# A store on SyncE's queue that waits for a load on GpSimd's queue (fp32 decoder layer, one core)

## What is computed

```python
x = _rmsnorm(hidden_states, ln_weight)
h_q = (x @ w_q.T).reshape(b, lq, H, DH)
h_k = (key_value_states @ w_k.T).reshape(b, lk, H, DH)
h_v = (key_value_states @ w_v.T).reshape(b, lk, H, DH)
score = jnp.einsum('bqhd,bkhd->bhqk', h_q, h_k)
...
attn = jnp.einsum('bhqk,bkhd->bqhd', score, h_v).reshape(b, lq, H * DH)
out = attn @ w_out.T
```

## Time and profile before

| | |
|---|---|
| timed runs | 1069.12, 1069.39, 1070.8 us; median 1069.39 |
| profiled execution, its own time | 1065.68 us |
| its span, first to last instruction | 1063.5 us |
| TensorE busy | 1025.7 us (96% of the span) |
| VectorE, ScalarE, GpSimd busy | 761.1, 500.7, 472.9 us |
| DMA | 158.72 MB, mean 149 GB/s |

### The profile page before, as it was taken

The page is one execution under the profiler, slowest core; times in us unless marked ns, Lnnn a source line. Parts: engine busy times, 40 slices in busy tenths (PEclk is TensorE's granted clock), DMA queues, the critical chain, the costliest instruction groups (busy, mean ns, idle before and its releaser), DMA issues.

```text
span 1063.5 us, 20567 instructions
## 1 busy us (share of the span) xinstructions
PE 1025.7 (96%) x6354; PEld 890.7 (84%) x6354; DVE 761.1 (72%) x2269; ACT 500.7 (47%) x1377; POOL 472.9 (44%) x568
## 2 busy tenths in 40 slices
PE   7899978999989999999999999999999999999998
PEld 6677766888878888898888888888888888888786
DVE  6799989674657675767767676767676767676784
ACT  4888886463434353444343434444343434353422
POOL 7576676599954242423334242424242424242052
PEclk9999999999999999999999999999999999999999
DMA  4302001144275647373736464646464655635102
GB/s 155 130 12 61 2 1 60 66 149 176 87 241 181 216 144 237 123 245 139 251 130 235 147 222 168 223 151 224 162 221 144 217 178 182 209 131 200 68 1 80
DMA packets 44844, 158.72 MB, mean 149 GB/s; under 512 B 4736, under 2 KB 21504, under 8 KB 32128
## 3 DMA queue, kind: packets, MB, share of 16 engines
q0 software_dynamic: 14240, 103.82, 28.1%
q1 hardware_dynamic: 30560, 54.37, 15.3%
HBM read 148.73 MB, written 9.44 MB: 149 GB/s over the span
## 4 chain that ended last, share of the span: by engine, by line
PE 78%; DVE 9%; issue 5%; POOL 4%; ACT 3%; DMA 1%; POOLq 0%; DVEq 0%; ACTq 0%
PE bank L1948 25%; PE bank L760 20%; PE bank L2110 16%; PE bank L2097 5%; PE bank L2080 5%; PE bank L2128 3%; PE bank L2087 2%; DVE sm L481 2%; POOL sm L322 1%; DMA ring<-block_sums 1%; ACT pr L410 1%; PE bank L2166 1%; DVE alpha L557 1%; PE bank L686 1%; ACT pr L1341 0%
## 5 line engine op out<-in xcount | busy, mean ns | idle before, releaser
L1341 ACT ACTIVATE pr<-sm,nmx 128x128 f32<-128x128 f32 x256 | 99.8, 391 | 174.5 <-DVE nmx L1597 174.4
L1048 POOL TENSOR_TENSOR bm<-mask,bias 128x512 f32<-128x512 f32 x64 | 84.6, 1323 | 160.7 <-DVE nmx L1597 158.1
L1647 DVE TENSOR_TENSOR acc<-acc,bank 128x512 f32<-128x512 f32 x128 | 86.2, 684 | 78.6 <-PE bank L2110 78.5
L1077 POOL TENSOR_TENSOR pool_gate<-eps 128x1 f32<-128x1 f32 x95 | 37.6, 396 | 234.5 <-PE bank L1948 234.5
L1948 PE MATMUL bank<-ring,wqk_hi 128*128 128x512 f32 x392 | 110.7, 404 | 3.4 <-DMA ring<-block_sums 2.2
L1615 DVE TENSOR_TENSOR wqk_lo<-qk_raw,wqk_hi 128x512 fp32r<-128x512 f32 x98 | 106.7, 1089 | 8.5 <-ACT wqk_hi L1371 8.5
L1334 ACT COPY v<-bank 128x256 f32<-128x256 f32 x124 | 45.9, 370 | 125.0 <-PE bank L760 78.0
L2110 PE MATMUL bank<-wo_hi,at_hi 128*128 128x512 f32 x256 | 100.5, 393 | 0.3 <-DVE acc L1647 0.3
L2110 PE MATMUL bank<-wo_hi,at_lo 128*128 128x512 f32 x256 | 100.0, 391 | 0.5 <-DVE at_lo L1609 0.5
L2110 PE MATMUL bank<-wo_lo,at_hi 128*128 128x512 f32 x256 | 100.0, 390 | 0.0
L760 PE MATMUL bank<-wv_hi,cT_hi 128*128 128x256 f32 x512 | 88.4, 295 | 0.2 <-DVE wv_lo L1903 0.2
(11 more groups left out here) (296 smaller groups left out, 2604.2 us busy)
## 6 DMA issues: line engine op xcount, KB each, us to landing
ring<-block_sums POOLq DMA_DIRECT2D x96, 1024.0 KB, 5.2
qk_raw<-in_wqk SPq DMA_DIRECT2D x56, 256.0 KB, 5.3
o_raw<-in_wo SPq DMA_DIRECT2D x16, 512.0 KB, 3.3
v_raw<-in_wv SPq DMA_DIRECT2D x15, 512.0 KB, 4.5
block_sums<-stage SPq DMA_DIRECT2D x6, 512.0 KB, 4.1
acc<-in_x POOLq DMA_DIRECT2D x1, 2048.0 KB, 8.0
qk_raw<-in_wqk SPq DMA_DIRECT2D x4, 512.0 KB, 5.3
bias<-in_bias SPq DMA_DIRECT2D x16, 128.0 KB, 2.1
```

The source lines that it names most:

```text
L1048: nc.gpsimd.tensor_tensor(bm[:, s % 2], mask[:, HALF * (s // HG):HALF * (s // HG + 1), :], bias[:, i:i + 1, :].broadcast_to([P, HALF, T]), ...
L1077: nc.gpsimd.tensor_tensor(pool_gate[:, BLOCKS.index(name):BLOCKS.index(name) + 1], eps[:, 0:1], eps[:, 0:1], ALU.add)
L1341: e = nc.scalar.activation(pr[:, s % 2, k], sm[:, s % 2, k], ACT.Exp, bias=nmx[:, s % 2, k:k + 1], accum_out=sums[:, s % 2, k:k + 1])
L1647: nc.vector.tensor_tensor(acc[:, b], acc[:, b], PX[b % 2][:], ALU.add).then_inc(s_acc, 1)
```

## The change

One wait is added on SyncE ahead of the store of S4q. `loaded(SEVEN, "S4k")` is 32: on `s_ring[0]` the load of S1k in group 2 counts 16 and the load of S4k in group 2 the next 16.

```diff
@@ -1012,6 +1012,7 @@
             load_bias(2)
             sp.wait_ge(s_wo, 2)
             load_o(2)
+            sp.wait_ge(s_ring[0], loaded(SEVEN, "S4k"))
             keep("S4q", *[f32(mem.ring[1][:, p].rearrange("p c n -> p (c n)")) for p in range(2)])
             with sp.Fori(SEVEN, NG - 1) as g:
                 sp.wait_ge(s_wv, g + 1)
```

## The result

The changed kernel took 1071.26 us in the median of 22 runs (1069.49 to 1074.05). In the same sessions the kernel before took 1067.45 us in 22 runs (1064.85 to 1070.8): 3.8 us more, a ratio of 1.0037 with an interval of 1.0029 to 1.0046. The three runs known at the prediction, with a median of 1069.39, lay in the upper half of the kernel before. The forecast was -0.2 us.

What follows compares the result with a forecast made beforehand. TensorE, busy 1025.7 of 1063.5 us, was taken to bound the kernel, so only its idle time counts. The terms -2.2 + 2.0 gave -0.2 us, or 1069.2 us for the median, with a range of 1067.5 to 1071.5.

Steps and rivals of the forecast that it cites:

- Steps 1 to 3: Group 2: S4k lands at 311.3, saving 2.2 us; the S4q store is kept at 316.0; S3q is issued at 316.2.
- step 3: GpSimd in group 2: its wait for the S4q store ends last, so S3q is issued at 316.2, 4.5 us later.
- Step 4: TensorE ahead of p7 of the queries: S3q takes 5.7 us, lands at 321.9, a new stall of +2.0 us.
- The count of bytes: Check on S3q's landing from bytes owed by the queues at 354 GB/s: 321.0 without blocks d and b, 322.5 with them.
- The Trainium skill's rule about whole packets: DMA engines alternate queues by whole packets; GpSimd's larger ones would give S3q most of them: 5.1 us, sum -0.8 us.
- A: Rival, S4q store then S3q load: longer round trip, S3q lands at 325.0, stall 5.1, sum +2.9, 1072.3 us; chance 0.08.
- B: Rival, load of S4k: it does not speed up and lands at 315.0; +3.5, 1072.9 us; chance 0.02.
- C: Rival, load of S3q: held until blocks a and c have landed; stall 2.5, sum +0.3, 1069.7 us; chance 0.10.
- D: Rival, p7 of the queries: finds S3q landed, the full gain of -2.2 to -2.3, 1067.1 us; chance 0.05.
- Steps 5 and 6: Group 2: S3k lands at 322.0 to 324.8, covered; SyncE's own loads come 6.3 us later each and cost nothing.

Runs made afterwards that it cites:

- the version without the wait: Kernel before with the value weights and blocks a and c of group 3 issued ahead of the store of S4q, no new wait; 1063.03 us, then 1063.87 us.
- the kernel with early weights: Changed kernel with the value weights and blocks a and c of group 3 issued ahead of the new wait; 1069.86 us, ratio 1.0018 to the kernel before.
- the filled kernel: Changed kernel with TensorE's group 2 written out and 20 extra matmuls ahead of the wait for S3q; 1068.57 us, ratio 1.0008 to the kernel before.
- its control: Changed kernel with TensorE's group 2 written out ahead of its loop and nothing else; 1072.18 us, ratio 1.0041 to the kernel before.

## Why the prediction was wrong

Steps 1 to 3 held to a few tenths. S4k landed after 5.21 us (5.2 forecast), at 311.0; TensorE's stall there went (-2.3 us; -2.2 forecast). The second store took 4.7 us (4.2 taken), kept at 316.1 (316.0). GpSimd's gate was released by the store's DMA, as step 3 has it; S3q was issued at 316.69, 0.5 us later than forecast: the gate started 0.16 us behind the landing, and from gate to issue it took 0.43 us instead of the 0.14 of the earlier trace rows.

**Step 4 failed, twice.** First in size: "I take 5.7" for the load of S3q. It took 7.76 and landed at 324.4, so that the stall was 5.0 us and not 2.0: 2.1 us of the miss is the load, 0.5 its later issue, 0.4 TensorE's earlier arrival (319.5, not 319.9). I had both ends in hand, 5.1 and 7.2, and weighed towards the shorter one because S3k had d and b beside it. But S3k had been issued 0.7 us ahead of them; here they were issued at 315.3 and 315.8, ahead of S3q, with the value weights, a and c still on the way. The rows fit this. A load of 1 MB issued 0.5 to 0.7 us ahead of d and b took 5.1 us in the kernel before and 5.4 and 5.3 in the two runs of the version without the wait, where d and b took 5.5 to 7.0. With d and b ahead, in the kernel with early weights, S3q took 7.0 us and d and b 2.9 and 3.5. In these rows whichever was issued first, on either queue, was hardly stretched. No run changed the order alone, so that it is the order is argued and not shown.

The runs say what each part is worth: alone or with S3k 5.1 to 5.2 us, with S3k, d and b 7.0, with all of it 7.8 (8.1 and 8.0 in the filled kernel and its control). The count of bytes ended at 322.5 because it held no bytes of S3k and of the bias: by the windows after, some 4.5 MB had moved by 324.4 (7.5 us at 329 GB/s, 4.9 at 424), against 3.7 counted. Whether S3k, which cost nothing by itself, cost part of the last 0.8 us among the others stays open: with all of SyncE's blocks and S3k held it was 7.1, but the store and the issue were later there. With the row of S3q before, 7.2, the stall would have been 3.5 us and the sum +1.3.

Second in kind: a stall was priced at its own length, and what the clock does behind it was put at nothing. Its price was 5.0 + 2.8 us, because the clock was down for most of the 7 us behind it. No row of before showed a fall after its 2.16 us stall, and I took that for "a stall costs what it lasts". The trace of before did hold a fall, at 154 us (0.57 in the mean of 4 us); the slices of the page are 26.6 us long and show it as a 9. The longer fall of the changed kernel is one 8 among the 9s of its page. So "90% or more in all 40 slices" did not mean a clock without falls.

The sum in the prediction's terms: -2.3 + 5.0 + 2.8 = +5.5 in the profiled execution, and +3.8 in the medians. That the medians differ by less would fit a fall of the clock behind the short stall in part of the executions of the kernel before, which its profiled one had not; this is argued, not counted. From the version without any stall at 1063.0 to 1063.9 us, adding 5.0 and 2.8 gives 1070.8 to 1071.7, and 1071.26 was measured.

The Trainium skill's rule about whole packets (DMA: Bandwidth & Descriptors, Queues, rings and completion order), as step 4 applied it, spoke for 5.1 us and for a smaller loss still. The rows decide against that here: 0.5 MB in SyncE's small packets cost S3q 1.9 us. Whether the profile's packets are the ones that the rule means, no run here shows.

**The rivals.** A, the longer round trip, is what happened: it had S3q landing at 325.0 (324.4), a sum of +2.9 and 0.08 of the chance. Its place was right. That its landing time came so close is partly luck: it took the store at 5.8 us (4.7) and the load at 7.2 (7.8), and the two misses partly cancel. It lacked the clock. B: S4k did speed up. C: its price did not arise, since block c landed at 319.5, long before S3q, so no row here tests its rule. D did not occur. The time itself, 1071.26, lies inside the range of 1067.5 to 1071.5, but that is luck: the range was built on a median of three runs 1.9 us above that of the 22, and built on 1067.45 it would have ended at 1069.6. The change lies clearly on the other side of the forecast.

**Steps 5 and 6.** S3k took 9.8 us, more than the 7.9 I allowed, and landed at 327.2, not by 324.8: the cover I gave it (wanted at 325.6) was gone. It made no one wait, since p7 of the keys had itself moved to 331.0, and in the run with full clock to 328.2. SyncE's blocks made ScalarE wait nowhere, as forecast.

## What to carry to other kernels

A wait that takes a store off a busy moment must be followed to whoever waits for the store: here a load was freed of 3.7 us, of which 2.2 counted, and the next load was made to start 5 us late and into the traffic that the wait had held back. Hold back the transfers with slack (the weights), or issue them earlier into an idle stretch, and let the one that others depend on go first. In group 2 a stall of TensorE of 3 us or more cost its length and 1.7 to 2.8 us on top; count that whenever a change moves idle time into one piece. And read the clock in windows of a few us, around every stall and elsewhere, before taking it as full.

## What was not expected of the hardware

- The clock falls within the stall or right behind it: after 5.61 us of idle time 2.3 us were lost, after 5.03 us 2.8, after 3.05 us 1.7, after 2.04 us 1.6 in one execution and none after 2.16 in another; after 1.14, 1.19 and 1.37 us none. But a short stall alone does not tell: in six of thirteen profiled executions it fell at 153 to 156 us, after waits of 0.8 to 1.4 us with work between them, and the other seven have the same waits without a fall. The Trainium skill (TensorE: Matmul & The Clock Gate, What's actually happening) names the two levels, 1.2 and 2.4 GHz; the 0.50 and 1.00 that the traces grant are these.
- Two loads of 1 MB on one queue, 0.7 us apart, took 5.1 and 8.0 us: the first was not slowed. 0.5 MB issued ahead of it on the other queue slowed the same load by 1.9 us; 0.5 MB issued just behind such a load left it at 5.1 to 5.4.
- The second of two 512 KB stores took 3.6 to 3.7 us with nothing behind it on its own queue, 4.7 to 4.8 with the value weights and blocks of weights behind it, with S4k beside it or without, and 6.1 once, which stays unexplained. The load that was taken away from beside it did not matter.
